# Four norms behind linears: units in another order, one root for two norms, the last tile's transposes in the next stage

## The chip, the cores and the metric

The kernel runs on one core of a Trainium2 chip. Its time is the device time of one execution in microseconds (us), given as the median of several runs. A profile of one further execution shows when each instruction ran on the engines: PE (matrix products and transposes), DVE (elementwise work and statistics), ACT (elementwise work with function tables), POOL (elementwise work), and SP, which issues the transfers from memory.

## The reference

625 tokens of width 768 pass through four layers, each made of a graph network, an attention-like mixer and a feed-forward or expert network, with a residual stream `x` in between. What matters here are four layer norms that stand right behind a linear layer whose result is added to a running sum:

```
y = x + h @ W                                   # 768 columns, three units of 256
n = (y - mean(y)) / sqrt(var(y) + eps)          # A: behind L1's mixer projection, for the router and experts
                                                # B: behind L1's experts' second matrices, for L2's GAT linear
n = n * gamma + beta                            # C: behind L2's mixer projection, for fc1
x1 = norm(x + ...; eps 1e-5, no gamma)          # D: behind fc2, two norms in a row:
n  = norm(x1; eps 1e-5) * gamma + beta          #    the layer's own, then the feed-forward's, for its in-projection
```

In D the second norm's variance is `var / (var + eps1)`, since the first norm has made the mean zero.

## The kernel before, in words

The program is a list of stages (`Stage`), planned once in Python; each stage emits its instructions into the five queues, and every engine works its own queue strictly in that order. Engines wait for each other by counters (`Ticks`): each instruction that matters adds one to its engine's counter, and the plan knows each value ahead.

Tokens come in 5 tiles of 125 (`NT`, `TP`). Weights come in units of 256 columns (768 KB), through a ring of three raw slots (`WSLOTS`); a unit's slot is free when the last product that reads it is done. Products are made in pairs of rounded numbers: ACT makes the high half of a unit (`split_high`, L270), POOL subtracts it in place to leave the low half (`split_low`, L277), and `products` (L58) issues 3 x 6 matmuls: high by low, low by high, high by high. High halves alternate between two places of their own (`Net.high`); a stage's units ask for the split of the unit two further on. Products go to 8 PSUM banks in turn, and a bank is free when its reader is done (`freed`).

`LinearNorm` does a linear and the norm behind it. PE: for each of three units, the products of the five tiles (`product`); with the last unit, `turn` (transposes, L957) of tile t behind the product of tile t + 1 (with `columns`) or t + 2 (without), and the remaining turns at the end. DVE, for each product: add to the running sum (L402) and partial statistics (L1041); with the last unit also mean and variance (L1045), then the inverse of ACT's root (L1049) and the scaling to `out` (L1060). In D (`first`) there is a second variance, root and inverse and a product of both (L1053 to L1057). ACT: the roots (L1091, L1094), and from the transposed tile in PSUM, in two groups of three chunks, the high half (L1083); with `columns` first three scale-and-bias copies (L1080), one for each chunk. DVE subtracts for the low half (`low`, L1011, L1017), and with `columns` does the last half tile itself (L1029 to L1021). `made` tells for each tile when its low half is written.

The next stage reads these pairs. `LinearT` (weights stationary, tokens moving) works each 128-column part of its weights in two halves of the tokens, `HALVES`: tiles 0 to 2 (375 tokens, taken as 376, so one token of tile 3 is read) and tiles 3 and 4 (250); only the first part waits, for `made[3]` and `made[4]`. `Linear` (tokens stationary) waits for one tile at a time. The router is a `LinearT` with one part of 8 columns. All of PE's work of one stage comes before that of the next, and so on every engine.

Of the kernel before, what the change touches and what calls it, by code (L numbers as in the profile page):

```python
# [16 lines left out]
TP = 125  # L17
# [82 lines left out]
class Net:  # L100


    def __init__(self, nc, ctx, ins):
        self.nc, self.ins = nc, ins
        sb = lambda name, shape, dt=F32: ctx.enter_context(nc.sbuf_tensor(name, shape, dt))
        sem = lambda name: ctx.enter_context(nc.semaphore(name))
        self.pe, self.act, self.dve, self.pool = (Ticks(sem(n)) for n in ("pe_done", "act_done", "dve_done", "pool_done"))
        self.const_landed, self.stored = sem("const_landed"), sem("stored")
        self.ps = ctx.enter_context(nc.psum_tensor("ps", [128, BANKS, 512], F32))
# [23 lines left out]
        self.high_made, self.low_made = sem("weights_high_made"), sem("weights_low_made")  # L133
        self.units, self.high_used, self.segment = [], [[], []], 0
        self.wsem = [sem(f"weights_landed{i}") for i in range(WSLOTS)]
# [3 lines left out]
        self.cols = sb("bias_cols", [128, 104])  # L139
        self.eps = {value: sb(name, [128, 1]) for name, value in (("eps5", 1e-5), ("eps8", 1e-8))}  # L140
        self.kv = sb("kv", [128, 24 * 65])
# [160 lines left out]
class Stage:  # L302
# [67 lines left out]
    def tensor(self, pe):  # L370
        pass
# [46 lines left out]
class LinearT(Stage):  # L418
# [4 lines left out]

    def __init__(self, net, xT, parts, evac="ad", after=None, tiles=None):
        super().__init__(net, after)
        self.xT, self.parts, self.tiles = xT, parts, tiles
# [20 lines left out]
    def chunk_done(self, m):  # L447

        return [self.net.freed[b] for b, _ in self.g[2 * m:2 * m + 2]]

    def tensor(self, pe):
        if self.tiles is None:
            self.begin(pe)
        kp, kc = self.xT.shape[0], self.xT.shape[1]
        i = 0
        for load, c0, w, out, bias, kind in self.parts:
            pe.wait_ge(self.net.low_made, load.unit + 1)
            weights = {"hi": load.high, "lo": load.dst}
            for t0, t1 in HALVES:
                b = self.g[i][0]  # L460
                if self.tiles is not None and i < 2:
                    pe.wait_ge(*self.tiles[min(t1, NT - 1)])
                if b >= BANKS:
                    pe.wait_ge(*self.free(b))
                n = (t1 - t0) * TP + (t1 - t0) * TP % 2
                mm = products(self.net, self.net.ps[:w, b % BANKS, 0:n], kc, lambda s, k: weights[s][:kp, k, c0:c0 + w],
                              lambda m, k: (self.xT.hi if m == "hi" else self.xT.lo)[:, k, t0 * TP:t0 * TP + n])
                mm.then_inc(self.net.pe.sem, self.net.pe.one())
                i += 1

    def last(self, i):

        return i % 2 == 1 and (i // 2 + 1 == len(self.parts) or self.parts[i // 2 + 1][0] is not self.parts[i // 2][0])

    def evac(self, eng, letter, ticks):
        self.begin(eng)
        for i, (b, e) in enumerate(self.g):
            load, c0, w, out, bias, kind = self.parts[i // 2]
            t0, t1 = HALVES[i % 2]
            ts, ps = slice(t0 * TP, t1 * TP), self.net.ps[:w, b % BANKS, 0:(t1 - t0) * TP]  # L480
            if self.pairs and letter == "a":
# [263 lines left out]
class Linear(Stage):  # L745

    def __init__(self, net, xT, units, evac="ad", after=None, rows=(), stats=None, tiles=None, coefs=None):
        super().__init__(net, after)  # L750
        self.xT, self.units, self.rows, self.stats, self.tiles, self.coefs = xT, units, rows, stats, tiles, coefs
        a = d = 0
# [113 lines left out]
class LinearNorm(Linear):  # L866
# [235 lines left out]
    def gpsimd(self, pool):  # L1102
        for load in self.weights:
            self.net.split_low(load.unit + 2, load.segment)

# [2069 lines left out]

def linear_T(net, xT, w, out, bias=None, kind="copy", rows=None, cols=None, evac="ad", after=None, tiles=None):
# [6 lines left out]
    return LinearT(net, xT, parts, evac, after, tiles)  # L3183

# [20 lines left out]

def linear(net, xT, w, out, kind="copy", add=None, rows=None, cols=None, bias=None, evac="ad", kp=128, after=None, stats=None, tiles=None, coefs=None):

    units = linear_units(net, w, out, kind, add, rows, cols, bias, kp)
    return Linear(net, xT, units, evac if kind in ("copy", "relu") else "d", rows=[bias] if bias else (), after=after, stats=stats, tiles=tiles, coefs=coefs)

# [170 lines left out]

def router(net, xT, w, logits, row=None, tiles=None):

    n = w.shape[1]
    out = net.asb[:n, :]
    scores = LinearT(net, xT, [(net.weights(w), 0, n, out, None, "copy")], tiles=tiles)
    scores.low_later = True
    ToTokens(net, out, logits, row)
    return scores.loads[0]
# [49 lines left out]
def network(net):  # L3439
# [139 lines left out]
    for i in range(2):  # L3579
        for s in range(2):  # L3580
# [28 lines left out]
    XT = pair(net.XT, G[5])  # L3609
    normed = linear_norm(net, pair(G[0], G[2]), ins["L1_mix_proj_wT"], R, tok(G[1]), XT, 1e-5, tiles=turned.made)  # L3610
# [4 lines left out]
    scored = router(net, XT, ins["L1_ffn_router_wT"], logits, tiles=normed.made)  # L3615
    chosen = TopTwo(net, logits, gates, "all", sel, None, scored)
# [9 lines left out]
    XT = pair(net.XT, G[4])  # L3626
    normed = linear_norm(net, hidden[1], experts_w2("L1_ffn_w2"), R, tok(G[5]), XT, 1e-5, rows=(D, 2 * D),
                         after=now() + [mark for ends in made[3:6] for mark in ends])
# [7 lines left out]
    biases2 = [net.into(net.kv[:, o:o + D].unsqueeze(1), ins[n].to_broadcast([128, D]).unsqueeze(1), start) for o, n in ((0, "L2_gnn_b2"), (D, "L2_mix_fc2_b"))]  # L3636
    linear(net, XT, w, hA, cols=(0, D), evac="a", tiles=normed.made, coefs=gat_coefs(net, hA, UNIT, 128, *[a[:, 0:D] for a in att], coef, G[2]))
    outB = G[1][:TP, 1280:2560].rearrange("p (t w) -> p t w", t=NT)
# [32 lines left out]
    XT = pair(net.XT, G[4])  # L3671
    normed = linear_norm(net, pair(G[1], G[2]), ins["L2_mix_proj_w"], tok(G[5]), tok(G[0]), XT, 1e-8, [norm_cols[n] for n in ("L2_mix_ln2_w", "L2_mix_ln2_b")],
                         after=now() + bias_p.ends(), tiles=turned.made)
    start = now()
    made, used = [], []
    for q in range(5):
        if q < 4:
            made.append(linear_T(net, XT, ins["L2_mix_fc1_w"], pair(G[q % 2], G[2 + q % 2]), bias=col["fc1_b_c"][:, 6 * q:6 * q + 6], kind="gelu",
                                 cols=(q * D, (q + 1) * D), evac="a", after=start if q < 2 else used[q - 2], tiles=None if q else normed.made))
# [5 lines left out]
    normed = linear_norm(net, pair(G[1], G[3]), ins["L2_mix_fc2_w"], R, tok(G[0]), XT, 1e-5, [norm_cols[n] for n in ("L2_ffn_ln1_g", "L2_ffn_ln1_b")], 1e-5,  # L3685
                         rows=(3 * D, 4 * D), after=start + made[3].ends() + added.ends())
# [4 lines left out]
    start = now()  # L3691
    linear_T(net, XT, w, feat(G[0]), bias=col["in_b_c"][:, 0:6], cols=(0, D), tiles=normed.made)
    linear_T(net, XT, w, feat(G[1]), bias=col["in_b_c"][:, 6:12], cols=(D, 2 * D), after=start)
# [212 lines left out]
```

## Time and profile before

| | us |
|---|---|
| median of 3 runs | 2921.95 (2920.42 to 2924.36) |
| profiled execution | 2924.71 |
| its span on the core | 2922.7 |
| PE busy | 2714.2 (93%) |
| DVE busy | 1417.6 (49%) |
| ACT busy | 1129.5 (39%) |
| POOL busy | 705.3 (24%) |

Times in the rows are from the span's start. A row of a timeline gives the start, the busy time of the instructions merged in it, the engine, the line of the kernel, what is written and read, and how many there are; in brackets the engine's idle time before it and what ended that. A line can be that of a helper: all products have L58, all adds L402. The clock of PE is given as a share of its full speed.

### The profile page before, as it was taken

What the parts mean: (1) busy time and instruction counts of PE and PEld (TensorE: products, weight loads), DVE (VectorE), ACT (ScalarE), POOL (GpSimd) and SP (SyncE); (2) the same over time, 40 slices, a digit from 0 to 9 for tenths busy, and PEclk for the clock granted to TensorE, in tenths of its full rate; (3) what the DMA queues carried; (4) which work ended last, traced back from release to release, by engine and by line L of the source; (5) the groups of instructions that cost most, each with busy time, mean ns of one, the idle gap of its engine ahead of it and who ended that gap; (6) DMA issues with size and microseconds to landing.
All of it is one profiled execution on the core that took longest, in us unless ns stands there. A gap on an engine that the chain in (4) does not pass through costs nothing. (4 is left out here: it accounts for less than half of the span.)

```text
span 2922.7 us, 48945 instructions
## 1 busy us (share of the span) xinstructions
PE 2714.2 (93%) x20003; PEld 2468.4 (84%) x20003; DVE 1417.6 (49%) x3608; ACT 1129.5 (39%) x2107; POOL 705.3 (24%) x261
## 2 busy tenths in 40 slices
PE   9999999997678999998899989989998899999899
PEld 9999999995338978998897989989768797797699
DVE  9777565564113135558842542240574664303743
ACT  7633255561003203328631253332463432355331
POOL 0144311110002321220224343323303332113032
PEclk9999999998898999999999999999999999999999
DMA  2022221016991211221021112222101221111022
GB/s 65 12 77 80 87 71 39 28 50 246 413 370 57 65 40 45 66 80 41 12 87 54 58 59 77 76 66 66 39 1 34 69 68 44 47 33 34 23 66 70
DMA packets 164572, 220.07 MB, mean 75 GB/s; under 512 B 21801, under 2 KB 144326, under 8 KB 164351
## 3 DMA queue, kind: packets, MB, share of 16 engines
q1 hardware_dynamic: 164350, 216.95, 22.5%
q8 instruction: 160, 2.62, 0.4%
q14 instruction: 62, 0.50, 0.1%
HBM read 215.00 MB, written 1.92 MB: 74 GB/s over the span
## 5 line engine op out<-in xcount | busy, mean ns | idle before, releaser
L58 PE MATMUL ps<-weights_r,buf_r 128*125 128x256 f32 (+3 forms) x4050 | 538.8, 284 | 5.9 <-DVE kv L2625 1.7
L277 POOL TENSOR_TENSOR weights_r<-weights,weights_r 128x1536 fp32r<-128x1536 f32 (+1 forms) x79 | 273.7, 3465 | 1039.1 <-ACT weights_r L270 1025.3
L58 PEld LDWEIGHTS ps<-weights_r,buf_r 128*125 128x125 f32 (+1 forms) x4050 | 508.3, 186 | 9.2 <-issue 4.2
L277 POOL TENSOR_TENSOR weights_r<-weights,head_weights_r 128x1536 fp32r<-128x1536 f32 (+1 forms) x77 | 270.4, 3511 | 1002.0 <-ACT head_weights_r L270 980.2
L58 PE MATMUL ps<-xT_r,weights_r 128*128 128x376 f32 (+1 forms) x2100 | 343.7, 309 | 0.0
L58 PE MATMUL ps<-head_weights_r,buf_r 128*125 128x256 f32 (+2 forms) x2310 | 316.6, 283 | 0.0
L58 PEld LDWEIGHTS ps<-xT_r,weights_r 128*128 128x128 f32 x2100 | 311.6, 187 | 4.8 <-issue 2.6
L58 PEld LDWEIGHTS ps<-head_weights_r,buf_r 128*125 128x125 f32 x2310 | 293.9, 187 | 0.0
L58 PE MATMUL ps<-weights_r,xT_r 128*125 128x256 f32 x1680 | 234.0, 283 | 8.0 <-issue 4.8
L270 ACT ACTIVATE head_weights_r<-weights 128x1536 fp32r<-128x1536 f32 (+1 forms) x77 | 112.8, 1465 | 306.3 <-PE ps L58 193.1
L58 PEld LDWEIGHTS ps<-weights_r,xT_r 128*125 128x125 f32 x1680 | 213.5, 187 | 10.4 <-issue 5.4
L1975 PE MATMUL ps<-buf,buf 125*125 125x192 f32 (+2 forms) x1100 | 208.6, 350 | 0.0
L270 ACT ACTIVATE weights_r<-weights 128x1536 fp32r<-128x1536 f32 (+1 forms) x79 | 114.6, 1451 | 231.4 <-PE ps L58 201.8
L1975 PEld LDWEIGHTS ps<-buf,buf 125*125 125x125 f32 x1100 | 165.1, 188 | 39.6
L389 ACT ACTIVATE buf<-ps 125x256 f32<-125x256 f32 (+5 forms) x221 | 83.1, 395 | 251.9 <-PE ps L58 251.7
L402 DVE TENSOR_TENSOR resid<-ps,resid 125x256 f32<-125x256 f32 (+1 forms) x165 | 72.8, 447 | 192.0 <-PE ps L58 173.8
L58 PE MATMUL ps<-buf_r,head_weights_r 128*128 128x376 f32 (+3 forms) x708 | 126.5, 316 | 12.3 <-issue 9.5
L58 PE MATMUL ps<-buf_r,weights_r 128*128 128x376 f32 (+2 forms) x744 | 130.0, 310 | 2.8 <-PE ps L58 1.1
L58 PEld LDWEIGHTS ps<-buf_r,head_weights_r 128*128 128x128 f32 (+2 forms) x708 | 109.7, 190 | 16.5 <-issue 11.5
L390 ACT ACTIVATE buf<-ps,bias_cols 128x375 f32<-128x375 f32 (+1 forms) x106 | 56.1, 536 | 170.8 <-PE ps L58 170.8
L1692 PE MATMUL ps<-buf,buf 125*125 125x313 f16 x800 | 112.6, 306 | 9.4 <-ACT buf L1713 9.4
L853 DVE CUSTOM_DVE_ANT_0 buf<-buf,row 125x128 f32<-125x128 f32 (+3 forms) x240 | 92.6, 441 | 58.7 <-ACT buf L389 53.1
(369 smaller groups left out, 4320.3 us busy)
## 6 DMA issues: line engine op xcount, KB each, us to landing
expert_regions<-in_L_ffn_w SPq DMA_DIRECT2D x64, 576.0 KB, 15.1
expert_regions<-in_L_ffn_w SPq DMA_DIRECT2D x48, 768.0 KB, 20.5
weights<-in_L_mix_fc_w SPq DMA_DIRECT2D x24, 768.0 KB, 4.5
weights<-in_L_gnn_W SPq DMA_DIRECT2D x18, 768.0 KB, 4.5
weights<-in_L_ffn_W SPq DMA_DIRECT2D x12, 768.0 KB, 4.7
weights<-in_L_mix_w_mapT SPq DMA_DIRECT2D x9, 768.0 KB, 4.7
weights<-in_L_gnn_W_out SPq DMA_DIRECT2D x9, 768.0 KB, 4.6
weights<-in_L_mix_kqv_wT SPq DMA_DIRECT2D x9, 768.0 KB, 4.6
```

The costliest lines, as they stand in the source:

```text
L58: mm = net.nc.tensor.matmul(ps, net.r(stationary(s, k)), net.r(moving(m, k)), start=(n == 0 and k == 0), stop=(stop and n == 2 and k == kc ...
L270: self.nc.scalar.activation(self.r(load.high), load.dst, ACT.Identity).then_inc(self.high_made, 1)
L277: self.nc.gpsimd.tensor_tensor(self.r(load.dst), load.dst, self.r(load.high), ALU.subtract).then_inc(self.low_made, 1)
L389: return nc.scalar.activation(out, ps, func)
L390: return nc.scalar.activation(out, ps, func, bias=bias)
L402: return nc.vector.tensor_tensor(out, ps, add, ALU.add)
L853: self.net.nc.vector.tensor_tensor_reduce(out=self.scratch[:TP, (n % 2) * HALF:(n % 2) * HALF + c1 - c0], in0=self.h[:, t, c0:c1], in1=sel ...
L1692: mm = self.nc.tensor.matmul(self.net.ps[:TP, b % BANKS, 0:self.HALF_SRC], self.hot_dst[c % self.DEPTH][:, t * TP:(t + 1) * TP], self.hot_ ...
L1975: mm = nc.tensor.matmul(self.ps(q, TP, self.w), self.PT[:, s, t * TP:(t + 1) * TP], self.heads[k][2][:, s, j * self.w:(j + 1) * self.w], s ...
```

## The change

The four norms A to D become stages of a new class, `PairedNorm`.

- Unit 0 is worked over all tiles as before. Then, tile by tile, come the products of units 1 and 2, and behind them the turn of the tile before.
- The turn of the last tile is not in the stage's own list: the next stage calls `turn_last` behind its first product (`LinearT`) or its second (`Linear`). It counts on a semaphore of its own.
- In D one root serves both norms: the scale of both together is the inverse of one root of `(1 + eps) * var + eps1 * eps`; the first norm's own inverse is made for all tiles at the end of the stage.
- The third unit's high half has a place of its own (in the second third of `P1`) and is made at the start of the stage; the two other places alternate by a counter of their own (`turns`).
- A `LinearT` with a `prior` takes 374 and 251 tokens instead of 375 and 250, so that its first half ends inside tile 2, and works the first halves of two parts before their second halves.
- One constant column more (`eps10`) is cleared at the start.

```diff
 class Net: split
-        slot = load.unit = len(self.units)
+        load.unit, slot = len(self.units), self.turns
+        self.turns += 1
...
 class LinearT: __init__, tensor
+        self.cut = 3 * TP - (prior is not None)
+        self.pieces = [(n, j) for n in range(len(parts)) for j in range(2)]
+        if prior:
+            ahead = min(2, len(parts))
+            self.pieces[:2 * ahead] = [(n, j) for j in range(2) for n in range(ahead)]
...
+            if self.tiles is not None and (j == 0 or part == 0):
+                pe.wait_ge(*self.tiles[2 if self.prior and j == 0 else 3 if j == 0 else 4])
...
+            if i == 0 and self.prior:
+                self.prior.turn_last(pe)
...
 class Linear: tensor
             self.product(pe, i, b)
+            if i == 1 and self.prior:
+                self.prior.turn_last(pe)
...
+class PairedNorm(LinearNorm):
+        last, halves = NT - 1, (0, 1)
+        columned = lambda t, g: [("column", t, g, c) for c in range(3 if columns else 0)] + [("high", t, g)]
+        for t in range(NT):
+            pe.append(("product", t))
+            dve += [("add", t), ("moments", t)]
+        for t in range(NT):
+            turned = [("low", t - 2, g) for g in halves] if t > 1 else []
+            pe += [("product", NT + t), ("product", 2 * NT + t)] + [("turn", t - 1, g) for g in halves if t > 0]
+            dve += [("add", NT + t), ("moments", NT + t)] + (turned if t == last else []) + [("add", 2 * NT + t), ("moments", 2 * NT + t), ("mean", t)]
+            dve += (turned if t < last else []) + [("inverse", t), ("norm", t)]
+            act.append(("root", t))
+            if t == 0:
+                act.append(("weights", 1))
+            if t > 0:
+                act += [q for g in halves for q in columned(t - 1, g)]
+        dve += [("low", last - 1, g) for g in halves]
+        if columns:
+            act += columned(last, 0)
+            dve += columned(last, 1) + [("low", last, 1), ("low", last, 0)]
+        else:
+            act += [q for g in halves for q in columned(last, g)]
+            dve += [("low", last, g) for g in halves]
+        act.append(("weights", 2))
+        if first:
+            act.append(("own root",))
+            dve.append(("own inverse",))
...
+        for load in self.weights[:2]:
+            net.split(load)
+        net.split_into(self.weights[2], net.P1[:, SLOT:2 * SLOT], self.after)
...
+            if kind == "root":
+                eps, scale = (self.first * self.eps, 1.0 + self.eps) if self.first else (self.eps, 1.0)
+                ins = nc.scalar.activation(self.scale[:, t:t + 1], mv[:, t, 1:2], ACT.Sqrt, bias=self.net.eps[eps][:TP, :], scale=scale)
...
 network: A, B, C, D
-    normed = linear_norm(net, ...)
+    normed = paired_norm(net, ...)
 and the stage behind each: prior=normed
```

On ACT `("weights", 1)` is the split of the next stage's first unit, `("weights", 2)` that of its second; the stage's own third unit is split ahead of the list.

## Rows read from the trace of the kernel before

**Rows 1.** The page's first part: span, then each engine's busy time.
```profile
span 2922.7 us, 48945 instructions
...
PE 2714.2 (93%) x20003; PEld 2468.4 (84%) x20003; DVE 1417.6 (49%) x3608; ACT 1129.5 (39%) x2107; POOL 705.3 (24%) x261
```

**Rows 2.** Waits of PE: total us, times, longest us.
```profile
PE ps L957 <- DVE buf L1060: 29.8, 16, 7.7
...
PE ps L957 <- ACT buf L1080: 6.9, 4, 2.5
```

**Rows 3.** Windows A to D: length, busy us per engine, clock, DMA share, GB/s.
```profile
1107.85:1152.81 44.96, 41.57 (x344) 38.97 (x343) 25.37 (x63) 13.00 (x26) 7.27 (x3) 1.00 0.15 38
1254.25:1304.40 50.15, 47.86 (x391) 47.46 (x391) 28.42 (x87) 13.63 (x25) 14.02 (x4) 0.97 0.26 85
1655.97:1712.25 56.28, 48.84 (x373) 47.96 (x373) 32.21 (x75) 25.77 (x55) 10.44 (x3) 0.94 0.14 43
1924.21:1985.11 60.90, 49.85 (x375) 48.57 (x373) 27.75 (x72) 25.11 (x54) 13.93 (x4) 0.92 0.17 53
```

**Rows 4.** PE's timeline in B and D: start, us, line, idle before.
```profile
1282.62 2.41 PE L58 MATMUL ps<-weights_r,buf_r 128*125 128x256 f32 x18
...
1285.42 2.38 PE L58 MATMUL ps<-weights_r,buf_r 128*125 128x256 f32 x18
...
1937.02 0.87 PE L58 MATMUL ps<-weights_r,buf_r 128*125 128x256 f32 x6
...
1939.15 0.88 PE L58 MATMUL ps<-weights_r,buf_r 128*125 128x256 f32 x6
```

**Rows 5.** Windows: the first half-part behind D.
```profile
1972.20:1977.80 5.60, 5.60 (x18) 5.60 (x19) 0.36 (x1) 0.33 (x1) 3.45 (x1) 0.52 0.00 0
```

**Rows 6.** PE's timeline behind D, second and third part.
```profile
1979.90 1.21 PE L58 MATMUL ps<-buf_r,head_weights_r 128*128 128x376 f32 x6
...
1983.03 0.86 PE L58 MATMUL ps<-buf_r,head_weights_r 128*128 128x250 f32 x6
...
1985.11 1.20 PE L58 MATMUL ps<-buf_r,weights_r 128*128 128x376 f32 x6
```

**Rows 7.** DVE's timeline in A, tile 0: add and scaling.
```profile
1131.58 0.42 DVE L402 TENSOR_TENSOR resid<-ps,resid 125x256 f32<-125x256 f32 x1 [1.24 <-PE ps L58]
...
1133.30 0.68 DVE L1060 TENSOR_SCALAR buf<-resid,stats 125x768 f32<-125x768 f32 x1
```

**Rows 8.** ACT's timeline at D's end.
```profile
1969.48 1.13 ACT L1080 ACTIVATE buf<-ps,bias_cols 128x125 f32<-128x125 f32 x3
...
1971.07 1.47 ACT L270 ACTIVATE weights_r<-weights 128x1536 fp32r<-128x1536 f32 x1
```

**Rows 9.** DMA issues in D: count, KB each, us to landing.
```profile
weights<-in_L_ffn_in_wT SPq DMA_DIRECT2D x4, 768.0 KB, 4.5
```

**Rows 10.** POOL's timeline in A, B and D: low halves.
```profile
1147.24 3.50 POOL L277 TENSOR_TENSOR weights_r<-weights,head_weights_r 128x1536 fp32r<-128x1536 f32 x1 [17.11 <-ACT head_weights_r L270]
...
1277.48 3.50 POOL L277 TENSOR_TENSOR weights_r<-weights,head_weights_r 128x1536 fp32r<-128x1536 f32 x1 [7.11 <-ACT head_weights_r L270]
...
1972.61 3.45 POOL L277 TENSOR_TENSOR weights_r<-weights,weights_r 128x1536 fp32r<-128x1536 f32 x1 [21.77 <-ACT weights_r L270]
```

**Rows 11.** DVE's timeline at D's end: the last half tile.
```profile
1969.17 1.04 DVE L1029 TENSOR_SCALAR buf<-ps,bias_cols 128x125 f32<-128x125 f32 x3 [0.82 <-PE ps L957]
...
1970.70 0.55 DVE L1021 TENSOR_TENSOR buf_r<-buf,xT_r 128x375 fp32r<-128x375 f32 x1
```

**Rows 12.** PE's timeline at A's end: last turn, router's second half.
```profile
1144.37 0.83 PE L957 MATMUL ps<-ident,buf 125*128 125x125 f32 x6 [1.70 <-DVE buf L1060]
...
1149.23 0.85 PE L58 MATMUL ps<-buf_r,weights_r 128*8 128x250 f32 x6
```

**Rows 13.** DVE's timeline in B: the first scaling.
```profile
1279.68 1.71 DVE L1060 TENSOR_SCALAR buf<-resid,stats 125x768 f32<-125x768 f32 x1
```

**Rows 14.** PE's timeline behind B: the GAT heads' first transposes.
```profile
1327.49 2.42 PE L1962 MATMUL ps<-ident,stats 125*125 125x125 f32 x20 [1.60 <-issue]
```

More of the change, by code:

```diff
@@ L447, in chunk_done, with span @@
     def chunk_done(self, m):
-        return [self.net.freed[b] for b, _ in self.g[2 * m:2 * m + 2]]
+        return [self.net.freed[self.g[self.pieces.index((m, j))][0]] for j in range(2)]
+    def span(self, j):
+        return ((0, self.cut), (self.cut, N))[j]
     def tensor(self, pe):
@@ L454, in tensor, with first @@
         kp, kc = self.xT.shape[0], self.xT.shape[1]
-        i = 0
-        for load, c0, w, out, bias, kind in self.parts:
+        for i, (part, j) in enumerate(self.pieces):
+            load, c0, w, out, bias, kind = self.parts[part]
             pe.wait_ge(self.net.low_made, load.unit + 1)
             weights = {"hi": load.high, "lo": load.dst}
[L459 to L469, printed above, removed]
+            b = self.g[i][0]
+            if self.tiles is not None and (j == 0 or part == 0):
+                pe.wait_ge(*self.tiles[2 if self.prior and j == 0 else 3 if j == 0 else 4])
+            if b >= BANKS:
+                pe.wait_ge(*self.free(b))
+            first = self.first(j)
+            n = self.span(j)[1] - first
+            n += n % 2
+            mm = products(self.net, self.net.ps[:w, b % BANKS, 0:n], kc, lambda s, k: weights[s][:kp, k, c0:c0 + w],
+                          lambda m, k: (self.xT.hi if m == "hi" else self.xT.lo)[:, k, first:first + n])
+            mm.then_inc(self.net.pe.sem, self.net.pe.one())
+            if i == 0 and self.prior:
+                self.prior.turn_last(pe)
+    def first(self, j):
+        return self.span(j)[0] - (self.cut % 2 == 0 and j == 1)
     def last(self, i):
-        return i % 2 == 1 and (i // 2 + 1 == len(self.parts) or self.parts[i // 2 + 1][0] is not self.parts[i // 2][0])
+        return not any(self.parts[part][0] is self.parts[self.pieces[i][0]][0] for part, j in self.pieces[i + 1:])
     def evac(self, eng, letter, ticks):
@@ L477, in evac @@
         for i, (b, e) in enumerate(self.g):
-            load, c0, w, out, bias, kind = self.parts[i // 2]
-            t0, t1 = HALVES[i % 2]
-            ts, ps = slice(t0 * TP, t1 * TP), self.net.ps[:w, b % BANKS, 0:(t1 - t0) * TP]
+            part, j = self.pieces[i]
+            load, c0, w, out, bias, kind = self.parts[part]
+            ts = slice(*self.span(j))
+            ps = self.net.ps[:w, b % BANKS, ts.start - self.first(j):ts.stop - self.first(j)]
             if self.pairs and letter == "a":
@@ L745, with __init__ @@
 class Linear(Stage):
-    def __init__(self, net, xT, units, evac="ad", after=None, rows=(), stats=None, tiles=None, coefs=None):
+    def __init__(self, net, xT, units, evac="ad", after=None, rows=(), stats=None, tiles=None, coefs=None, prior=None):
         super().__init__(net, after)
+        self.prior = prior
         self.xT, self.units, self.rows, self.stats, self.tiles, self.coefs = xT, units, rows, stats, tiles, coefs
@@ L3173, in weight_units, with linear_T @@
     return [net.weights(w[r0:r1, c:min(c + UNIT, c1)]) for c in range(c0, c1, UNIT)]
-def linear_T(net, xT, w, out, bias=None, kind="copy", rows=None, cols=None, evac="ad", after=None, tiles=None):
+def linear_T(net, xT, w, out, bias=None, kind="copy", rows=None, cols=None, evac="ad", after=None, tiles=None, prior=None):
     parts, m = [], 0
@@ L3203, in linear_units, with linear, paired_norm @@
     return units
-def linear(net, xT, w, out, kind="copy", add=None, rows=None, cols=None, bias=None, evac="ad", kp=128, after=None, stats=None, tiles=None, coefs=None):
+def linear(net, xT, w, out, kind="copy", add=None, rows=None, cols=None, bias=None, evac="ad", kp=128, after=None, stats=None, tiles=None, coefs=None, prior=None):
     units = linear_units(net, w, out, kind, add, rows, cols, bias, kp)
-    return Linear(net, xT, units, evac if kind in ("copy", "relu") else "d", rows=[bias] if bias else (), after=after, stats=stats, tiles=tiles, coefs=coefs)
+    return Linear(net, xT, units, evac if kind in ("copy", "relu") else "d", rows=[bias] if bias else (), after=after, stats=stats, tiles=tiles, coefs=coefs, prior=prior)
+def paired_norm(net, xT, w, x, out, outT, eps, columns=None, first=None, rows=None, after=None, tiles=None):
+    return PairedNorm(net, xT, linear_units(net, w, x, "add", x, rows), x, out, outT, eps, columns, first, after, tiles)
 def linear_norm(net, xT, w, x, out, outT, eps, columns=None, first=None, rows=None, kp=128, after=None, tiles=None, more=None, early=None):
@@ L3379, in gated_experts, with router @@
     return done
-def router(net, xT, w, logits, row=None, tiles=None):
+def router(net, xT, w, logits, row=None, tiles=None, prior=None):
     n = w.shape[1]
     out = net.asb[:n, :]
-    scores = LinearT(net, xT, [(net.weights(w), 0, n, out, None, "copy")], tiles=tiles)
+    scores = LinearT(net, xT, [(net.weights(w), 0, n, out, None, "copy")], tiles=tiles, prior=prior)
     scores.low_later = True
@@ L3614, in network @@
     start = now()
-    scored = router(net, XT, ins["L1_ffn_router_wT"], logits, tiles=normed.made)
+    scored = router(net, XT, ins["L1_ffn_router_wT"], logits, tiles=normed.made, prior=normed)
     chosen = TopTwo(net, logits, gates, "all", sel, None, scored)
@@ L3678, in network @@
             made.append(linear_T(net, XT, ins["L2_mix_fc1_w"], pair(G[q % 2], G[2 + q % 2]), bias=col["fc1_b_c"][:, 6 * q:6 * q + 6], kind="gelu",
[L3679 removed]
+                                 cols=(q * D, (q + 1) * D), evac="a", after=start if q < 2 else used[q - 2], tiles=None if q else normed.made, prior=None if q else normed))
         if q == 0:
@@ L3691, in network @@
     start = now()
-    linear_T(net, XT, w, feat(G[0]), bias=col["in_b_c"][:, 0:6], cols=(0, D), tiles=normed.made)
+    linear_T(net, XT, w, feat(G[0]), bias=col["in_b_c"][:, 0:6], cols=(0, D), tiles=normed.made, prior=normed)
     linear_T(net, XT, w, feat(G[1]), bias=col["in_b_c"][:, 6:12], cols=(D, 2 * D), after=start)
```

155 lines of the change are left out of this document (145 added, 10 removed).

## The prediction

> **What bounds the kernel now.** The page first: PE is busy 93% of the span [rows 1], so the time is PE's own stream plus its waits. The chain of waits on the page reaches back only over the last quarter of the span; the four changed stages lie before it, so I go by PE's waits instead. Among PE's longest waiters stand the transposes of L957, which wait for the norm's scaling on DVE (L1060, 29.8 us in 16 waits), or behind ACT's scale-and-bias copies (L1080, 6.9 us) [rows 2]. Then the timelines of the four stages, of which I call A the norm in front of the L1 router, B the one in front of the L2 GAT linear, C the one in front of fc1, D the one in front of the in-projection. For each I take the stretch from its first product to a point where PE flows again: in A the first expert product, in B the second unit of the next linear, in C and D the third 128-column part of the next one. These take 44.96, 50.15, 56.28 and 60.90 us [rows 3].
>
> What they would take without a wait follows from two rows: product to product is 2.13 us, product to product with one tile's six transposes between is 2.80, so a turn costs 0.66 [rows 4]. The wait is in the tail: after the last product nothing is left for PE but two turns, the norm chain of the last tile, and ACT's and DVE's copies, all one after the other. In C and D that leaves PE idle so long that the next stage's first half-part runs at a granted clock of 0.52, i.e. at the 1.2 GHz level: 5.60 us for 18 matmuls [rows 5], where the same 18 take 1979.90 to 1983.03, 3.13 us, a little later, and the narrower second half 2.08 [rows 6].
>
> **The change, part by part.** Write T0 for the start of product 0 and T for the end of product 14.
>
> *Order of the products.* Unit 0 runs over all tiles as before; units 1 and 2 run tile by tile, a turn one tile late. By T: 15 x 2.13 + 3 x 0.66 = 33.93 us. Does a turn wait for its norm? From the add to the end of the scaling DVE took 1131.58 to 1133.98, 2.40 us [rows 7], 0.2 behind the product, and with two lows ahead of the inverse some 1 us more: 3.6. PE works two products and a turn, 4.9, before it asks for it. ACT has per tile a root and two groups of three columns and a copy; one group takes 1.59 (1969.48 to 1971.07) [rows 8], so 3.4 of 4.9. DVE has that chain, a second add with its moments (0.9) and two lows (1.0): 4.3 of 4.9. So no waits here; before, PE waited in D for each tile, since tiles ended every 2.13.
>
> *Weights.* The third unit's high half goes to a place of its own and is made first on ACT. Its raw load in B and D is released only at T0 and lands 4.5 us later [rows 9]; ACT 1.5 and POOL 3.5 [rows 8, 10] make it ready by about T0 + 10, and product 10 asks at T0 + 6 x 2.13 = 12.8. Cost: from nothing to one POOL pass, 3.5 per stage; I take nothing, as the gap is 2.7. The next stage's first unit is split after root 0, its raw slot free at T0 + 10.65: ready by about T0 + 22. The next stage's second unit is released later than before, by product 9 (T - 2.1), and lands at T + 2.4, before ACT gets to it. On SP only the later weights stand behind that wait.
>
> *One root in D.* Two DVE operations, one root, one reciprocal and a multiply per tile go. They were in the tail; in the new order they would lie beside products, so the gain is already in "no wait" and I add nothing.
>
> *The late turn, B.* After T: turn 3, products 0 and 1 of the next linear, turn 4, products 2 to 4. Norm 4 ends at T + 2.6, turn 4 starts at T + 4.9; low 3 and low 4 come some 3 us before their products. 33.93 + 2 x 0.66 + 5 x 2.13 = 45.90 against 50.15: **4.25 us saved**.
>
> *The late turn, C and D.* After T: turn 3 (0.66), first half of part 0 (3.13), turn 4 (0.66), first half of part 1 (3.13): PE is through at T + 7.6. ACT: root 4 near T + 1.7, then both groups of tile 3 and the first of tile 4, done at T + 1.85 + 3 x 1.59 = 6.6. DVE: the second group of tile 3 is there at T + 5.1; its low 0.5, columns and copy of the last half 1.53 (1969.17 to 1970.70) [rows 11], two lows 0.47 + 0.55: T + 8.2. The second halves ask for exactly that, so a new wait of about 0.65 (0 to 1.5) takes the place of the old ones; too short to cost the clock, as in A a wait of 1.70 did not: 5 us behind it six matmuls still took 0.85 [rows 12]. Then 2 x 2.08: T + 12.4. POOL begins the next unit's low 1.54 after ACT begins its high [rows 8, 10], at T + 8.15, and is done at 11.6, before it is asked for. Sum 33.93 + 12.41 = 46.34: **C saves 9.94, D 14.56**. The cut of the columns moves from 376 + 250 to 374 + 252: the same sum, no cost.
>
> *The late turn, A.* The router has one part only, so one half (3.13) covers turn 4. PE would then wait for low 4 until about T + 5.8, and by 1149.23 to 1152.81 (second half to experts, 3.58) [rows 12] be at the experts at T + 9.4. But their weights are later: turn 4 starts at T + 3.8; in the trace the turn of 1144.37 was followed by POOL's low at 1147.24, 2.87 later, for 3.50 [rows 10, 12]: T + 10.2. 33.93 + 10.2 = 44.1 against 44.96: **0.85 saved** (-0.5 to 2.5), so the second wait hides most of A's gain.
>
> *The rest.* One more cleared column stands at the start, beside the landing inputs: nothing, at most one add's 0.42 [rows 7]. The parity of the high slots changes order only.
>
> Sum: 0.85 + 4.25 + 9.94 + 14.56 = 29.6. The profiled execution took 2924.71 us (its span 2922.7 and 2.0 around it), 2.8 above the runs' median of 2921.95. From it: 2895.1; on the median **2892.5 us**.
>
> **A rule that speaks against it.** A scaling on DVE that began while POOL was making a low half took 1.71 us and ended 0.4 after POOL did, against 0.68 alone [rows 7, 10, 13]. The Trainium skill, SBUF — State Buffer, in its part on contention within the engine side, says that DVE and GpSimd share a pair of ports under an exclusive lock: whichever starts first holds it for its whole instruction, and a DVE operation with two inputs in SBUF is among those that wait. With that rule the trace agrees. What that row would do here: the last low of C and D reads SBUF alone, like that scaling, and starts at T + 7.6, 0.5 before POOL's at T + 8.15. If POOL came first, the sum would be the second case below.
>
> **The rivals.**
> 1. *Forecast*, 2892.5 (2888 to 2897). For: C's and D's idle time lies wholly in what the order does away with.
> 2. *POOL overtakes DVE in the tail of C and D.* The last low then ends at 11.6 + 0.55 = T + 12.2, 4.0 later, and PE, idle that long, runs a half-part at the lower clock, 2.47 dearer: 2 x 6.47 = 12.9, **2905**. Against: both chains start from the same ACT copy, so the 0.5 doesn't drift.
> 3. *The next stage's second unit (or the third unit) is late*: a POOL pass of 3.5 in each stage, 14 us: **2906**. For: it is so in A already, and in B to D there is less than 1 us to spare. Against: nothing on ACT or POOL stands between.
> 4. *Gains of A and B are given back* at the next join: the GAT heads waited 1.60 us on DVE's coefficients after the linear [rows 14], and with the ACT evacuations now starting late DVE may set the end. 5.1 lost: **2897.5**.
> 5. *It doesn't do what it says*: the waits reappear in full elsewhere, since some transfer or DVE chain sets the time of the stretches behind: **2922**. Against: PE is busy 93%.
> 6. *Slower*: the norms come late for every turn. It decides once a norm is more than 1.3 us behind my 3.6, for instance if POOL blocks it again and again; PE then waits at every tile and its clock falls as in D's tail. Ten products at half speed cost 10 x 2.13 = 21.3 more per stage, 85 in all, less the 29.6: **2977**. Against: one POOL pass per stage falls among the norms, one tile long.
>
> **How the numbers follow.** Forecast 0.70, rival 2 0.07, 3 0.07, 4 0.10, 5 0.03, 6 0.03. Range 2886 to 2907: it takes in 1 to 4, and with the bounds of A and of the third unit leaves out about 1 in 10. A difference under 0.2%, 5.8 us, can't be told from none here. Faster 0.94 (1 to 4), same 0.03, slower 0.03.
>
> **What would show it.** In the changed profile: no wait of transposes for the scaling within the tiles; D's stretch near 46 us, as long as C's; clock 1.00 at the start of fc1 and of the in-projection; one wait of 0.5 to 1 us on DVE's low in front of the second halves; in A the first expert product waiting for POOL; and no DVE scaling of several us but one or two. I would be wrong if PE showed waits at turns in the middle of a stage, if the last low stood at 3.5 us beside POOL, or if the wait in front of the GAT heads grew by 4 us.

## The result and the profile after

The changed kernel takes **2898.9 us** (2897.05 to 2903.16, 4 runs) against 2921.87 for the kernel before (4 runs beside it). The ratio is 0.9913, 95% interval 0.9901 to 0.9924, which is 25.4 us (22 to 29); the two medians differ by 23.0. The forecast, 2892.5, is a ratio of 0.9899: direction and range hold, and the gain is some 4 us smaller than its 29.4 by the ratio, 6 by the medians. Two runs in a slow state, one of 4012 and one of 7779 us, stand in none of the ratios here and below.

The profiled execution took 2899.39 us. The page's first part, answering to [rows 1]: PE's work is as long as before, within 3 us, and the span 25.4 us shorter.

```profile
span 2897.3 us, 49066 instructions
...
PE 2711.2 (94%) x20003; PEld 2467.0 (85%) x20003; DVE 1418.9 (49%) x3603; ACT 1128.7 (39%) x2103; POOL 706.7 (24%) x261
```

The waits of PE, answering to [rows 2] (total us, times, longest us). L978 is the old order's transposes, which four norms outside the change still use. The new order's turns (L1195) don't appear: no turn within a stage waits for a norm. "Issue" means that the profile names nothing that the engine waited for.

```profile
PE ps L978 <- DVE buf L1081: 14.5, 6, 7.7
...
PE ps L58 <- issue: 11.1, 7, 4.8
...
PE ps L978 <- ACT buf L1101: 3.0, 2, 2.5
```

The windows of the four stretches, cut at the same two instructions as [rows 3]: 44.96, 50.15, 56.28 and 60.90 have become

```profile
1108.04:1152.26 44.22, 41.41 (x344) 39.00 (x343) 25.87 (x67) 13.53 (x27) 7.25 (x3) 1.00 0.18 42
1255.18:1301.06 45.88, 45.88 (x390) 45.88 (x391) 26.44 (x62) 13.18 (x25) 14.02 (x4) 1.00 0.28 92
1654.40:1700.99 46.59, 46.02 (x372) 45.66 (x373) 34.77 (x78) 25.94 (x55) 10.73 (x3) 1.00 0.16 52
1913.09:1959.58 46.49, 45.95 (x375) 45.60 (x373) 25.37 (x62) 23.98 (x50) 13.99 (x4) 1.00 0.23 69
```

Forecast were 44.1, 45.90, 46.34 and 46.34. PE is busy in all of B, and the clock is 1.00 in all four.

The tail of D on PE (start, us, line; in brackets the idle time before). The late turn at 1950.79 lies between the two first halves, and one wait of 0.54 is left, in front of the second halves, which start 0.10 behind the end of DVE's last low:

```profile
1949.75 1.20 PE L58 MATMUL ps<-xT_r,head_weights_r 128*128 128x374 f32 x6
1950.79 0.81 PE L1195 MATMUL ps<-ident,buf 125*128 125x125 f32 x6
1951.36 1.28 PE L58 MATMUL ps<-buf_r,head_weights_r 128*128 128x374 f32 x6
...
1955.24 0.95 PE L58 MATMUL ps<-buf_r,head_weights_r 128*128 128x252 f32 x6 [0.54 <-issue]
```

DVE there: the last two lows end at 1955.14. POOL's low of the next unit begins at that moment, 1.55 behind the start of ACT's high half for it (1953.59).

```profile
1949.15 0.68 DVE L1248 TENSOR_SCALAR buf<-resid,stats 125x768 f32<-125x768 f32 x1
...
1953.67 0.42 DVE L1258 CAST xT_r<-buf 128x375 fp32r<-128x375 f32 x1
1954.13 1.01 DVE L1266 TENSOR_TENSOR buf_r<-buf,xT_r 128x375 fp32r<-128x375 f32 x2
```

```profile
1955.14 3.49 POOL L279 TENSOR_TENSOR weights_r<-weights,weights_r 128x1536 fp32r<-128x1536 f32 x1 [20.51 <-ACT weights_r L272]
```

A's tail on PE, and POOL's low of the experts' weights. The experts begin at 1152.26, 0.25 after that low has ended, as forecast; the profile puts the wait down to DVE, and the experiment on A's bound below shows that it is POOL's. Two further waits stand shortly in front of it, and the twelve matmuls behind all three take 3.63 us, where the same twelve can take 2.23:

```profile
1147.87 0.85 PE L58 MATMUL ps<-buf_r,head_weights_r 128*8 128x252 f32 x6 [1.34 <-issue]
...
1150.87 0.68 PE L2935 MATMUL ps<-ident,a_src_rows 8*125 8x8 f32 x5 [0.76 <-DVE a_src_rows L395]
1152.26 1.46 PE L58 MATMUL ps<-buf_r,weights_r 128*128 128x376 f32 x6 [0.71 <-DVE stats L3240]
1153.52 3.63 PE L58 MATMUL ps<-xT_r,weights_r 128*128 128x376 f32 x12
```

```profile
1148.55 3.46 POOL L279 TENSOR_TENSOR weights_r<-weights,weights_r 128x1536 fp32r<-128x1536 f32 x1 [23.35 <-ACT weights_r L272]
```

**Where the rest went.** The stretches gave 0.74 + 4.27 + 9.69 + 14.41 = 29.1 us, the span only 25.4. The missing part lies in code that nobody changed, in two places above all: right behind A (1.5 us) and at the tail of the GAT heads behind B (1.65 us). At the second PE has the same three waits in both kernels. Before:

```profile
1430.75 2.75 PE L1410 MATMUL ps<-ident,buf 125*128 125x125 f32 x24 [0.60 <-PE ps L1975]
1434.62 3.16 PE L1410 MATMUL ps<-ident,buf 125*128 125x125 f32 x16 [1.12 <-DVE buf_r L1428]
1439.08 1.09 PE L58 MATMUL ps<-weights_r,buf_r 128*125 128x192 f32 x8 [1.30 <-DVE buf_r L1428]
1440.01 1.91 PE L58 MATMUL ps<-head_weights_r,buf_r 128*125 128x192 f32 x16
```

After, the same waits, and then sixteen matmuls in 3.28 instead of 1.91; the window behind the third wait (after first, before second) has a granted clock of 0.75 instead of 1.00, part of it at the 1.2 GHz level.

```profile
1427.54 2.75 PE L1615 MATMUL ps<-ident,buf 125*128 125x125 f32 x24 [0.60 <-PE ps L2180]
1431.42 3.16 PE L1615 MATMUL ps<-ident,buf 125*128 125x125 f32 x16 [1.12 <-DVE buf_r L1633]
1435.88 1.40 PE L58 MATMUL ps<-weights_r,buf_r 128*125 128x192 f32 x8 [1.30 <-DVE buf_r L1633]
1437.08 3.28 PE L58 MATMUL ps<-head_weights_r,buf_r 128*125 128x192 f32 x16
```

```profile
1435.88:1442.81 6.93, 6.93 (x48) 6.93 (x49) 6.47 (x17) 0.00 (x0) 6.85 (x5) 0.75 0.00 0
```

```profile
1439.08:1445.98 6.90, 6.90 (x63) 6.90 (x64) 6.44 (x17) 0.00 (x0) 6.82 (x5) 1.00 0.00 0
```

### The profile page after: what moved, and what is told of

It is laid out like the page before. It is cut to its first block and busy times, and to the rows that moved or that the text cites. A ratio compares the mean times of both kernels' runs of the same rounds, so it can differ in the third digit from the quotient of the medians.

```text
span 2897.3 us, 49066 instructions
## 1 busy us (share of the span) xinstructions
PE 2711.2 (94%) x20003; PEld 2467.0 (85%) x20003; DVE 1418.9 (49%) x3603; ACT 1128.7 (39%) x2103; POOL 706.7 (24%) x261
## 5 line engine op out<-in xcount | busy, mean ns | idle before, releaser
L279 POOL TENSOR_TENSOR weights_r<-weights,head_weights_r 128x1536 fp32r<-128x1536 f32 (+2 forms) x80 | 276.2, 3453 | 1040.2 <-ACT head_weights_r L272 1007.8
L279 POOL TENSOR_TENSOR weights_r<-weights,weights_r 128x1536 fp32r<-128x1536 f32 x76 | 269.5, 3545 | 974.0 <-ACT weights_r L272 974.0
L58 PE MATMUL ps<-xT_r,weights_r 128*128 128x376 f32 (+4 forms) x2028 | 333.8, 309 | 0.0
L58 PEld LDWEIGHTS ps<-xT_r,weights_r 128*128 128x128 f32 (+1 forms) x2028 | 303.2, 189 | 3.2 <-issue 2.2
L272 ACT ACTIVATE head_weights_r<-weights 128x1536 fp32r<-128x1536 f32 (+2 forms) x80 | 114.8, 1435 | 254.7 <-PE ps L58 134.5
L272 ACT ACTIVATE weights_r<-weights 128x1536 fp32r<-128x1536 f32 x76 | 112.7, 1483 | 218.3 <-PE ps L58 185.3
L58 PE MATMUL ps<-buf_r,head_weights_r 128*128 128x376 f32 (+7 forms) x780 | 138.3, 314 | 9.0 <-issue 5.2
L58 PEld LDWEIGHTS ps<-buf_r,head_weights_r 128*128 128x128 f32 (+3 forms) x780 | 117.6, 185 | 15.1 <-issue 7.9
L58 PE MATMUL ps<-xT_r,head_weights_r 128*128 128x376 f32 (+5 forms) x732 | 127.0, 309 | 0.0
L392 ACT ACTIVATE buf<-ps,bias_cols 128x375 f32<-128x375 f32 (+3 forms) x106 | 56.0, 536 | 161.0 <-PE ps L58 160.6
```

What stands on the lines that cost most here:

```text
L58: mm = net.nc.tensor.matmul(ps, net.r(stationary(s, k)), net.r(moving(m, k)), start=(n == 0 and k == 0), stop=(stop and n == 2 and k == kc ...
L272: self.nc.scalar.activation(self.r(load.high), load.dst, ACT.Identity).then_inc(self.high_made, 1)
L279: self.nc.gpsimd.tensor_tensor(self.r(load.dst), load.dst, self.r(load.high), ALU.subtract).then_inc(self.low_made, 1)
L392: return nc.scalar.activation(out, ps, func, bias=bias)
```

## The experiments

Each has the changed kernel as its base; the kernels of one group ran on one chip and share the runs of the kernel before.

**Which site pays.** A site is put back like this:

```diff
-    normed = paired_norm(net, ...)
+    normed = linear_norm(net, ...)
 and the stage behind it:
-    ... tiles=normed.made, prior=normed
+    ... tiles=normed.made
```

A alone (B, C, D put back):


> Only norm A is a PairedNorm with the late turn; B, C and D are as before. Theory (the gain of A is used up by two new waits and by the clock falling behind them): within 1.5 us of the kernel before, on either side, and the first expert product runs at the 1.2 GHz level in the profile, or if the clock stays up some 0.8 us are gained. Rival (A gains its 0.85 us or more, and what is missing of the forecast is lost elsewhere): 0.8 to 2.5 us faster, experts at full clock.

B alone:


> Only norm B is changed. Theory (each norm's gain stays): 4.3 us faster than before, 3 to 5.5. Rival (B's gain is given back at the GAT heads behind its linear, which wait for DVE): under 2 us faster, and the wait in front of the heads' first transposes, 1.6 us before, is 3 us or more longer.

C and D:


> Only C and D are changed. Theory (additive, nothing given back behind them): 24.1 us faster than before, 22 to 26, so all of the changed kernel's gain or a little more than it. Rival (part of C's and D's gain is given back in the 900 us behind them): 17 to 20 us faster, and some wait behind D is longer than before by that much.

B, C and D (A put back):


> A is left as before, B, C and D are changed. Theory (A is worth nothing or costs a little): 28.4 us faster than before, 26 to 30, that is 1 to 5 us faster than the changed kernel. Rival (A is worth 0.85 or more): 0.8 us or more slower than the changed kernel, 22 us faster than before.

Measured against the kernel before, in 5 rounds:

| | us | ratio (95%) |
|---|---|---|
| A alone | 2927.54 | 1.0008 (0.9999 to 1.0017) |
| B alone | 2924.27 | 1.0000 (0.9991 to 1.0008) |
| C and D | 2902.59 | 0.9924 (0.9911 to 0.9937) |
| B, C and D | 2899.25 | 0.9919 (0.9905 to 0.9933) |

C and D carry the gain: 22 us of their forecast 24.5. A is worth nothing that can be timed, and neither is B, though its stretch is 4.2 us shorter in its trace too. So the theory held for C and D only. With B alone it forecast 3 to 5.5 us and none came (at most 2.6 by the interval); the rival's sign was absent too, since the wait in front of the heads' first transposes is 1.60 as before. B, C and D should have gained 28.4 and gained 23.7 (20 to 28). A alone came out 2.3 us slower (5.0 slower to 0.3 faster), against a theory of within 1.5.

**The parts of the new order.** First the late turn is taken back: units tile by tile, but the last turn at the end of the stage itself, in all four sites.

```diff
+        pe += [("turn", last, g) for g in halves]
         dve += [("low", last - 1, g) for g in halves]
 and no stage behind it has a prior
```

> As the changed kernel in all four norms, but the last tile's turn stands at the end of its own stage and the next stage works its parts in the old order and cut: the tile-by-tile order alone. Theory (order and late turn each carry a part): PE waits for norm 4 from T + 0.7 to T + 2.9 and in C and D again for the low of tile 3 until T + 5.7; B 2 to 3 us longer than in the changed kernel, C and D 3.6 to 6 each, A the same: 9 to 15 us slower than the changed kernel, 10 to 16 faster than before. Rival (the order is all, the late turn covers what nobody waits for): within 3 us of the changed kernel.

Measured: 2914.01 us, 0.9964 (0.9951 to 0.9978, 3 rounds), some 15 us behind the changed kernel. PE at D's end, where two waits stand again, and the first half-part runs partly at the lower level (2.22 us for six matmuls that take 1.21 later):

```profile
1957.80 0.83 PE L1194 MATMUL ps<-ident,buf 125*128 125x125 f32 x6 [2.18 <-DVE buf L1244]
1960.60 2.22 PE L58 MATMUL ps<-buf_r,head_weights_r 128*128 128x376 f32 x6 [1.97 <-issue]
```

Between the same instructions of PE the stretches are 2.1 (B), 5.9 (C) and 5.2 us (D) longer than in the changed kernel, and A's is the same. (A's together with what lies behind it: 65.03 and 65.14, the clock fallen in both.) The theory holds. So the late turn, with the order of halves in the next stage that goes with it, gives some 13 of the 29 us in the stretches; the order tile by tile gives the rest, D's single root included, which is about 10 us in the timed runs.

Then D makes two roots and two inverses per tile again:

```diff
-  [("inverse", t), ("norm", t)]
+  [("inverse", t), ("var2", t), ("inverse2", t), ("both", t), ("norm", t)]
   act: ("root", t)
+  act: ("root2", t)
```

> As the changed kernel, but D makes two roots again, with the second variance, second inverse and product of both for each tile. Theory (in the new order these lie beside products; only the last tile's chain is 1.3 us longer, of which 0.9 was cover): D's stretch 0.4 to 1 us longer, no waits at the other turns. Rival (the single root carries a part of the gain): about 0.85 us for each of five tiles, D's stretch 3 to 4 us longer.

Measured: 2900.85 us, 0.9917 (0.9902 to 0.9932): no difference to the changed kernel that can be timed. In the trace D is 2.0 us longer, between the theory's 0.4 to 1 and the rival's 3 to 4: PE waits in front of the first half-part too, 1.06 us that the changed kernel does not have, and 1.11 instead of 0.54 in front of the second halves. The first half-part needs the low half of tile 2. With two roots that low ends at 1944.32, 0.10 ahead of it. In the changed kernel it ends just as close ahead, but PE is not idle there, so there was next to nothing to spare. With two roots:

```profile
1944.42 1.27 PE L58 MATMUL ps<-buf_r,head_weights_r 128*128 128x374 f32 x6 [1.06 <-issue]
...
1952.86 0.95 PE L58 MATMUL ps<-buf_r,head_weights_r 128*128 128x252 f32 x6 [1.11 <-issue]
```

```profile
1943.77 0.55 DVE L1275 TENSOR_TENSOR buf_r<-buf,xT_r 128x375 fp32r<-128x375 f32 x1 [0.86 <-ACT xT_r L1315]
```

The changed kernel, PE and DVE:

```profile
1947.61 1.27 PE L58 MATMUL ps<-buf_r,head_weights_r 128*128 128x374 f32 x6
```

```profile
1946.96 0.55 DVE L1266 TENSOR_TENSOR buf_r<-buf,xT_r 128x375 fp32r<-128x375 f32 x1 [0.59 <-ACT xT_r L1303]
```

So the single root is worth about 2 us in D's tail, more than I expected of this run.

**The bound in A.** ACT splits the next stage's second unit ahead of the last tile's copies, in A and B:

```diff
+            act.append(("weights", 2))
             act += [q for g in halves for q in columned(last, g)]
```

> As the changed kernel, but in A and B ACT makes the high half of the next stage's second unit before, not after, the last tile's high halves. Theory (in A the experts wait for POOL's low half, 10.2 us behind T): that low is done near T + 7.7, the first expert product starts at T + 9.4, A 0.8 us shorter, B unchanged; if the shorter wait keeps the clock up, A is up to 2.4 us shorter. Rival (POOL isn't what the experts wait for, but the router's chain): A unchanged within 0.2 us.

Measured: 2897.58 us, 0.9907 (0.989 to 0.9923). POOL's low indeed starts 1.43 before PE's second half now, where it had started 0.68 behind it, and PE no longer stops in front of the experts:

```profile
1149.47 0.86 PE L58 MATMUL ps<-buf_r,head_weights_r 128*8 128x252 f32 x6 [1.67 <-issue]
...
1153.08 1.31 PE L58 MATMUL ps<-buf_r,weights_r 128*128 128x376 f32 x6
```

```profile
1148.04 3.47 POOL L279 TENSOR_TENSOR weights_r<-weights,weights_r 128x1536 fp32r<-128x1536 f32 x1 [21.57 <-ACT weights_r L272]
```

But the wait in front of the second half grew from 1.34 to 1.67, since the last tile's copies are later by the split. With the clock up in both, A and what lies behind it take 63.17 us against 63.60 in the kernel with two roots: 0.4 us: neither the theory's 0.8 or more nor the rival's 0.2 or less, though the theory's cause is right. It is a version as good as the changed kernel, and no better one by these runs.

**Rival 2 made to happen.** The same edit in C and D, so that POOL's low starts ahead of DVE's last half tile:

```diff
         if columns:
+            act.append(("weights", 2))
             act += columned(last, 0)
```

> As the changed kernel, but in C and D ACT makes the high half of the next stage's second unit ahead of the last tile's first half, so that POOL's low begins near T + 6.6, ahead of DVE's copy and last two lows. Theory (DVE operations that read SBUF alone wait until POOL is through): DVE's copy or a low takes some 3 us, the second halves start near T + 11.6 and not T + 8.3, and PE's clock falls behind that wait: C and D 3.4 to 6 us longer each, 7 to 12 us slower than the changed kernel. Rival (no such wait, only ACT is 1.5 us later): 0.6 us longer each, under 2 us in all.

Measured: 2910.75 us, 0.9952 (0.9937 to 0.9967), 10 to 13 us behind the two kernels above, timed beside it. POOL's, DVE's and PE's timelines in D, and a window of PE's second halves:

```profile
1957.72 3.44 POOL L279 TENSOR_TENSOR weights_r<-weights,weights_r 128x1536 fp32r<-128x1536 f32 x1 [18.91 <-ACT weights_r L272]
```

```profile
1957.84 3.60 DVE L1259 CAST xT_r<-buf 128x375 fp32r<-128x375 f32 x1
```

```profile
1962.59 1.62 PE L58 MATMUL ps<-buf_r,head_weights_r 128*128 128x252 f32 x6 [3.71 <-issue]
```

```profile
1962.59:1969.67 7.08, 7.08 (x36) 7.08 (x37) 0.61 (x1) 1.04 (x2) 0.00 (x0) 0.57 0.00 1
```

The CAST, 0.42 in the changed kernel, began 0.12 behind POOL's start and took 3.60, until 0.28 after POOL's end. PE then waits 3.71 and runs the two second halves at a granted clock of 0.57. In C the wait is 3.72. The stretches grow by 4.5 (C) and 5.9 us (D). So rival 2 was a real danger at about the price named, 12.9 against 10.4 in the two stretches. In the changed kernel DVE's last low has just ended when POOL starts, 1955.14 for both in D, 1696.59 and 1696.61 in C: the distance is about the length of that low, the half us by which the prediction saw it start ahead.

**Chance or order?** Do the clock's falls in unchanged code belong to a kernel? Four runs: the first, second and fourth are kernels already profiled, unchanged; the third, with B alone, makes two products of the next linear twice:

```diff
+            for again in range(2 if self.prior and i in (11, 12) else 1):
                 mm = products(...)
```

> The kernel before, unchanged, in a second profile. Theory: whether PE's clock falls behind a group of short waits is not settled by the kernel; it differs from one execution to the next. Then the ratio to the kernel before holds 1 (0.9985 to 1.0015), and the second profile differs from the first by whole falls of 1.6 us each at one or more of these places: behind A (stretch 64.35 us with the clock up, 65.86 fallen), the tail of the GAT heads (74.74 or 76.4), the stretch behind it (45.06 or 46). Rival: the falls belong to the order of the instructions, and the second profile repeats 64.35, 74.74 and 45.06 within 0.1 us.

> The kernel with B alone changed, unchanged, in a second profile. Theory as for the kernel before: the stretch of B stays at 47.6 us (51.8 before), the tail of the GAT heads, 77.97 in its first profile, may come out at 74.7 or 76.4, and the ratio lies about 0.9986 if the gain of 4.2 us is kept (0.9976 to 0.9996). Rival: B's earlier end makes the clock fall in the tail of the GAT heads every time; then 76.4 or more again, and the ratio is 0.9995 to 1.0005.

> B alone changed, and two products of the next linear (its units 2, tiles 1 and 2) are made twice, which gives the same numbers: PE's work behind B grows by 2 x 2.13 = 4.26 us without a wait, about what B's stretch gained. If what lies behind is only moved along, this is 4.3 us slower than B alone (ratio to it 1.0015) and as long as the kernel before within 0.1 us in the sum of both stretches. If the fall of the clock in the tail of the GAT heads hangs on how early PE comes there, it is back at 74.74 us and the kernel is only 1 to 3 us slower than B alone.

> The changed kernel, unchanged, in a second profile. Theory: stretches B, C and D repeat within 0.1 us (47.5, 49.35, 49.4); A is 65.1 with the clock fallen or 63.6 with it up; the other places (tail of the GAT heads, behind it, 700 to 905 us) differ by whole falls of the clock; ratio 0.990 to 0.993. Rival: every stretch repeats within 0.1 us, so that the lost 4 us belong to the new order.

Measured: the kernel before again 2924.43 us, 0.9990 (0.9981 to 0.9998) against itself; B alone 0.9999 (0.9988 to 1.0010); B with two products twice 0.9994 (0.9986 to 1.0003); the changed kernel 2901.14, 0.9916 (0.9902 to 0.9929). The first shows how far such intervals can be trusted: 0.1% is no difference here. The stretches of PE, in us between the same two instructions by their place in PE's stream (with B and two products twice, the 36 added matmuls are counted off):

```
                      before        A alone  B alone       B, two   after
                      1st    2nd             1st    2nd    twice    1st    2nd
A and behind it       64.35  64.37  65.12    65.84  64.35  65.64    65.14  65.12
B and behind it       51.80  51.81  51.80    47.63  47.63  47.64    47.53  47.53
GAT linear and heads  94.27  94.31  94.26    94.23  94.23  98.48    94.39  94.39
tail of the heads     74.74  74.75  76.38    77.97  76.38  74.73    76.39  76.38
behind the tail       45.06  45.04  46.29    45.88  44.98  44.82    45.00  45.07
```

The kernel before and the changed kernel repeat all five within 0.1 us, as their rivals had it. B alone does not, though its tail fell both times, as its rival had it. Two things follow. A's clock falls or stays up in one and the same kernel: B alone has 65.84 and 64.35 there. Over all profiles, the old A is up in three (64.35 to 64.37) and fallen in four (65.64 to 65.88), the new A up in two (63.60, 63.17) and fallen in five (65.03 to 65.14). At equal clock the new A is 0.75 shorter, which is the trace's 0.74 and nearly the forecast's 0.85. The kernel with two roots shows the new A with the clock up row by row, with the waits of the changed kernel and no fall:

```profile
1144.99 0.85 PE L58 MATMUL ps<-buf_r,head_weights_r 128*8 128x252 f32 x6 [1.34 <-issue]
...
1149.38 1.29 PE L58 MATMUL ps<-buf_r,weights_r 128*128 128x376 f32 x6 [0.71 <-DVE stats L3252]
1150.50 2.23 PE L58 MATMUL ps<-xT_r,weights_r 128*128 128x376 f32 x12
```

In the old A the fall comes earlier, at the router's first matmuls, behind the waits of 1.70 and 0.95. These waits are the same to 0.01 in all seven profiles of it; the six matmuls then take 1.19 to 1.21 in three and 2.03 or 2.04 in four. First C and D alone, then the kernel before:

```profile
1144.47 0.83 PE L978 MATMUL ps<-ident,buf 125*128 125x125 f32 x6 [1.70 <-DVE buf L1081]
1146.25 2.04 PE L58 MATMUL ps<-buf_r,weights_r 128*8 128x376 f32 x6 [0.95 <-issue]
```

```profile
1146.15 1.19 PE L58 MATMUL ps<-buf_r,weights_r 128*8 128x376 f32 x6 [0.94 <-issue]
```

The tail of the heads is another matter. It fell in all nine profiles with the new B (76.37 to 78.02), and in one of four with the old B. With 4.26 us of products put in behind the new B, which brings PE there about when it came before, it is at 74.73 again. From B on, its four stretches sum to 265.67 us, against 263.22 for B alone (second profile): 4.26 us of added work cost 2.45. So the fall there goes with an early arrival of PE, with much the same waits: of B's 4.2 us, 1.65 are given back.

The arrival alone does not decide, though. The one fall with the old B is in A alone, where PE comes to the tail as far behind B's first product as in the kernel before (146.06 and 146.07 us) and finds the same waits, 0.60, 1.12 and 1.30. Its window behind the third wait, to be compared with the two above:

```profile
1440.70:1447.60 6.90, 6.89 (x48) 6.90 (x49) 6.44 (x17) 0.00 (x0) 6.82 (x5) 0.75 0.00 0
```

The return to 74.73 rests on one kernel with a shift, in which the first two waits are 0.69 and 1.03 instead of 0.60 and 1.12. That the earlier arrival causes the fall is likely, not shown; what decides stays open. It stays open, too, whether the timed runs keep the rest of B's gain: 2.6 us are 0.09%, within what the kernel before differs from itself.

## Why the prediction was right, and where it was short

1. *No waits within the tiles*: right, no L1195 among the waits.
2. *B*, 45.90: measured 45.88, and PE never idle.
3. *C and D*, 46.34 each: 46.59 and 46.49. The new wait, 0.65, is 0.56 and 0.54. The clock is 1.00 through both, where the half-part of [rows 5] had 0.52. The outcome is right, but the reason given for it, that a wait of 1.70 in A did not cost the clock, was luck of one profile: behind that same wait, and one of 0.95, the clock fell in four of seven profiles of the old A. Behind the new waits of C and D it did not: in five profiles with both as in the changed kernel C took 46.53 to 46.59 us and D 46.42 to 46.49.
4. *A*, 44.1: 44.22. "The second wait hides most of A's gain" is what the trace shows, and an earlier split uncovers only 0.4 us.
5. *Weights*: no unit of the four stages was late, and in B to D no unit behind them. Rival 3 falls.
6. *One root*: valued at nothing. Taking it back costs 2.0 us in D's stretch. That gain is part of D's 14.56; what failed is the reason, since two roots would not have lain beside products: the low half of tile 2 then comes late for the first half-part, which waits 1.06.
7. *Rival 2*: did not occur, and could have. All twenty scalings of the four norms took 0.68 to 0.89 us. Made to happen, it cost about what was named, and a CAST was held up like the scaling of [rows 13]: 3.60 us against 0.42. The Trainium skill, SBUF — State Buffer, in its part on contention within the engine side, names two kinds of DVE operations that POOL locks out, those in a two-port mode and those with two inputs in SBUF; with the lock the trace agrees. The row of the CAST names one input, so only the first kind would be left for it; no run here shows that mode.
8. *Rival 4* has nearly the time that was measured (2897.5) by the wrong mechanism. Its outcome, no time gained by A and B, is what A alone and B alone show, but the wait in front of the heads' first transposes is 1.60 in both kernels [rows 14]:

```profile
1324.15 2.42 PE L2167 MATMUL ps<-ident,stats 125*125 125x125 f32 x20 [1.60 <-issue]
```

**The step that was mis-sized** is the sum: each term was read in its own stretch and added to the whole time, as if everything behind were only moved along. The stretches gave 29.1 of 29.6. Of the 3.7 us that did not reach the span, 1.65 are the tail of the heads, where PE now comes earlier and the clock falls; 1.5 are A's clock, up in both profiles of the kernel before but falling in either order, so this part is chance; the rest is spread. The clock was weighed only at the new waits of C and D and from one profile, and not at unchanged waits further on. How much unchanged code moves by itself: the stretch from PE's first instruction to about 905 us took 896.5 to 900.8 us in the fourteen profiles. (On the median the prediction's own sum is 2921.95 - 29.6 = 2892.35, not 2892.5.)

## What to carry to other kernels

Put the last tile's chain behind the next stage's first work rather than at the end of its own: that gave nearly half of what the stretches gained here, for two transposed groups moved and the next stage's halves reordered. Before moving a POOL pass earlier, look at which DVE operations on SBUF then begin inside it. A fall of the clock costs some 1.5 us here, and it can come some 135 us behind the edit at waits that were there all along, so check a second profile of both kernels before calling a gain of that size real.

## What the runs showed that was not expected

- Identical waits, different clock: 0.60, 1.12 and 1.30 us in front of the same matmuls, which then took 1.91 or 3.28; at the new A 1.34, 0.76 and 0.71, then 2.23 or 3.63; at the old A 1.70 and 0.95, then 1.19 or 2.04. The tail of the heads did the same in the second profile of each of three kernels (up twice, or fallen twice), A's end in two of three.
- Two products made twice, 4.26 us of PE work, can't be seen in the timed result: 0.9994 (0.9986 to 1.0003) against 0.9999 (0.9988 to 1.0010) without them. Of the 1 to 3 us expected in between, 1 or 2 would be hidden by such intervals.
